# Gate loops of a fused graph network kernel: sigmoids in SBUF, two PSUM parts, query rows in PSUM

## The reference, cut to what matters

```python
def _gate(h, q, Wg, bg, Wq, bq):
    h3 = h.reshape(B, N, F)
    hg = jnp.einsum('bnf,gf->bng', h3, Wg[:, :F])
    qg = jnp.einsum('blf,gf->blg', q, Wg[:, F:]) + bg
    attn = jax.nn.sigmoid(hg[:, :, None, :] + qg[:, None, :, :])
    qi = jnp.einsum('bnlf,blf->bnf', attn, q)
    alpha = jax.nn.sigmoid(h3 @ Wq[:, :F].T + qi @ Wq[:, F:].T + bq)
    return (alpha * jnp.tanh(qi) + (1.0 - alpha) * h3).reshape(B * N, F)
```

## Time and profile before

| | |
|---|---|
| runs (3) | 1467.73 us median, 1459.67 to 1469.58 |
| the profiled execution | 1458.04 us, of it 1456.3 us span |
| TensorE matmul, busy | 1358.1 us (93%) |
| VectorE, busy | 986.9 us (68%) |
| ScalarE, busy | 773.1 us (53%) |
| GpSimd, busy | 207.3 us (14%) |
| mean granted TensorE clock | 0.974 |

### The profile page before, as it was taken

One profiled execution on the slowest core, in us unless ns is written; L12 is line 12 of the kernel. 1 busy time (PEld: TensorE's weight loads), 2 busy tenths in 40 slices (PEclk: granted clock), 3 DMA queues, 4 the chain that ended last, 5 costly groups with the idle time before them and its releaser, 6 DMA issues.

```text
span 1456.3 us, 24087 instructions
## 1 busy us (share of the span) xinstructions
PE 1358.1 (93%) x10014; PEld 1157.0 (79%) x10014; DVE 986.9 (68%) x1790; ACT 773.1 (53%) x1248; POOL 207.3 (14%) x103
## 2 busy tenths in 40 slices
PE   9999999999999798798789999789999999987998
PEld 8999433899533696588688999769899999986976
DVE  8745777645777756657667767776777677677455
ACT  3446888535888354344554654534455544445333
POOL 0110876000776100102001000001000000000100
PEclk9999999999999999999999999999999999998999
DMA  8456353146364222035325453063455555151100
GB/s 350 112 204 199 96 173 110 66 142 188 103 188 120 76 93 93 0 131 189 115 72 201 163 176 140 23 240 119 152 187 166 193 196 176 53 211 60 55 1 22
DMA packets 30835, 194.81 MB, mean 134 GB/s; under 512 B 4211, under 2 KB 4339, under 8 KB 14726
## 3 DMA queue, kind: packets, MB, share of 16 engines
q1 hardware_dynamic: 30726, 193.27, 39.0%
HBM read 183.03 MB, written 3.93 MB: 128 GB/s over the span
## 4 chain that ended last, share of the span: by engine, by line
PE 71%; DVE 17%; ACT 6%; POOL 3%; issue 2%; DMA 0%; DVEq 0%; SPq 0%; ACTq 0%; POOLq 0%
PE PS L358 55%; PE PS L978 6%; PE PS L987 5%; DVE WL L301 3%; PE PS L363 3%; POOL WK L1173 2%; PE PS L619 1%; POOL WL L308 1%; PE PS L460 1%; DVE SM L1345 1%; DVE SM L535 1%; DVE WK L1755 1%; ACT WH L294 1%; DVE WK L1760 1%; ACT GS L481 1%
## 5 line engine op out<-in xcount | busy, mean ns | idle before, releaser
L301 DVE TENSOR_TENSOR WL<-w,WH 128x768 fp32r<-128x768 f32 x373 | 354.6, 962 | 209.6 <-ACT WH L294 206.8
L294 ACT ACTIVATE WH<-w 128x768 fp32r<-128x768 f32 x381 | 315.5, 840 | 265.4 <-PE PS L358 252.3
L358 PE MATMUL PS<-XS,WH 128*128 128x256 f32 x2292 | 419.6, 286 | 13.0 <-DVE XS L485 7.1
L358 PEld LDWEIGHTS PS<-XS,WH 128*128 128x128 f32 x2292 | 357.2, 191 | 17.1 <-issue 11.1
L358 PE MATMUL PS<-XS,WL 128*128 128x256 f32 x1146 | 324.8, 283 | 0.0
L358 PEld LDWEIGHTS PS<-XS,WL 128*128 128x128 f32 x1146 | 218.5, 191 | 0.0
L1111 DVE TENSOR_TENSOR WK<-PS,WK 128x1024 f32<-128x1024 f32 x128 | 156.6, 1224 | 55.5 <-ACT PS L1055 54.5
L1173 POOL TENSOR_TENSOR WK<-WK 128x1024 f32<-128x1024 f32 x64 | 152.9, 2393 | 207.4 <-ACT WK L1052 207.4
L358 PE MATMUL PS<-WH,GS 128*128 128x256 f32 x864 | 159.0, 283 | 4.6 <-issue 1.4
L1055 ACT ACTIVATE PS<-PS 128x1024 f32<-128x1024 f32 x128 | 129.3, 1011 | 34.4 <-PE PS L978 34.3
L358 PEld LDWEIGHTS PS<-WH,GS 128*128 128x128 f32 x864 | 134.4, 188 | 7.3 <-issue 4.1
(11 more groups left out here) (253 smaller groups left out, 2014.2 us busy)
## 6 DMA issues: line engine op xcount, KB each, us to landing
w<-f2W_in SPq DMA_DIRECT2D x40, 1152.0 KB, 5.4
w<-Wrel_in SPq DMA_DIRECT2D x12, 1152.0 KB, 7.9
WK<-qrep_in SPq DMA_DIRECT2D x16, 768.0 KB, 5.5
w<-f1Wi_in SPq DMA_DIRECT2D x8, 1152.0 KB, 6.6
w<-f1Wo_in SPq DMA_DIRECT2D x8, 1152.0 KB, 5.1
w<-f3Wqkv_in SPq DMA_DIRECT2D x6, 1152.0 KB, 13.7
RT<-qg_rows SPq DMA_DIRECT2D x16, 384.0 KB, 6.2
RT<-AS SPq DMA_DIRECT2D x32, 192.0 KB, 6.6
```

Source lines behind the costliest of these rows:

```text
L294: A.e.activation(w_hi(i), w_raw(i), ACT.Copy).then_inc(*hi("w", i))
L301: V.e.tensor_tensor(w_lo(i), w_raw(i), w_hi(i), ALU.subtract).then_inc(*lo("w", i))
L358: ins = T.e.matmul(o, l, r, start=i == 0 and first, stop=i == n - 1 and last, skip_group_check=lint)
```

## The change

- The select parts get two places in PSUM instead of three: banks 4, 5 and 6, 7 in turn, `(3 * p + q) % 2`. A place is free as soon as ScalarE's sigmoid has read it.
- All three sigmoids write SG in SBUF. VectorE multiplies parts 0 and 2 in place there.
- VectorE's query rows lie in PSUM (GP, banks 2 and 3). For every group TensorE's new `spread(b)` fills them: two matmuls of 512 columns from QR, 64 partitions of XS (the two halves of 32 query rows), with the left side PK[0:64, 0:128]. It waits for VectorE's last product of the group before; VectorE's first product of a group waits for it.
- The split query rows come from DRAM (`query_rows`). Once, in the first graph layer, SyncE waits for the 32 stores, loads `qsel` (128 x 2048), ScalarE makes the upper half behind the aggregates of relation 2 and VectorE the lower, each one instruction, and SyncE stores them in 16 stores. This stands in `adj_sync`, ahead of `gate_sync` in the queue.
- The group's GQ load shrinks to GpSimd's 512 columns, and one load of QR is added.
- TensorE's order in the loop becomes select 0, sums unit 0, select 1, sums unit 1, select 2, and the spread of a group comes after select 2 of its first pair.

```diff
@@ -578,6 +579,7 @@
         qh, ql = (v[:, :].rearrange("p (k n) -> p k n", k=6) for v in (AS, XS))
         qgf = wk(14336, m=4, f=768)
         qgs = QS[:, :].rearrange("p (a m f) -> p a m f", a=2, m=4)
+        qss, qsx = QS[:, 0:4096].rearrange("p (a n) -> p a n", a=2), wk(4096, n=2048)
         Cr = wk(6144, r=3, m=2, n=256)
         Cj = wk(6144, j=6, n=256)
         Cn = wk(7680, n=512)
@@ -602,6 +604,15 @@
                         L.e.dma_start(qgr[2 * m + g // 2, a, :, g % 2, :],
                                       qgs[32 * g:32 * g + 32, a, m, :].bitcast(F32)).then_inc(*qg_out())
             qg_out.also("qg")
+            L.wait_ge(qg_out, "qg")
+            L.e.dma_start(qsx, dr["qsel"]).then_inc(*qs_in("qs"))
+            for a in range(2):
+                L.wait_ge(*((act, "upper", "qs"), (vec, "lower", "qs"))[a])
+                for g in range(4):
+                    for j in range(2):
+                        L.e.dma_start(qsr[4 * j + g, a, :, :],
+                                      qss[32 * g:32 * g + 32, a, 1024 * j:1024 * (j + 1)].bitcast(F32)).then_inc(*qs_out())
+            qs_out.also("qs")
 
         def adj_pe():
             b = bank_at(7, ("wake",), (pe, "wake"))
@@ -759,9 +770,11 @@
         NSG = 3
         SG = [wk(at, u=2, n=1536) for at in (0, 3072, 14336)]
         PARTS = [((0, 0), (0, 512)), ((0, 1024), (1, 1024)), ((1, 0), (1, 512))]
-        SP = [PS[:, 1024 * (1 + i):1024 * (2 + i)] for i in range(3)]
+        SP = [PS[:, 1024 * (2 + i):1024 * (3 + i)] for i in range(2)]
+        GP = PS[:, 1024:2048]
         GR = [RT[:, 1536 * i:1536 * (i + 1)] for i in range(2)]
-        GQ = [wk(11264 + 1536 * i, n=1536) for i in range(2)]
+        GQ = [wk(11264 + 512 * i, n=512) for i in range(2)]
+        QR = [XS[0:64, 1024 * (1 + i):1024 * (2 + i)] for i in range(2)]
         HG = AS[:, :].rearrange("p (a m f) -> p a m f", a=2, m=2)
         QA = wk(7680, n=384)
         QI = ((0, 224), (224, 256))
@@ -857,6 +870,8 @@
             for f in range(0, 6, 2):
                 aggregate(2, f)
             if n == "1":
+                A.wait_ge(qs_in, "qs")
+                act_upper(qss[:, 0, :], qsx, "qs")
                 A.wait_ge(pool, "counts")
                 A.e.activation(Cn, Cn, ACT.Ln).then_inc(*act())
                 A.e.activation(LD, LD, ACT.Ln).then_inc(*act("logs"))
@@ -895,6 +910,8 @@
             vec_gemm(t0, 12)
             for f in range(0, 6, 2):
                 aggregate(2, f)
+            if n == "1":
+                vec_lower(qss[:, 1, :], qsx, qss[:, 0, :], "qs")
             vec_gemm(t0, 24, None, 12)
             for f in range(6):
                 if f == 2:
@@ -916,9 +933,11 @@
             def queries(b):
                 if before(b) is not None:
                     o, d = before(b)
-                    for q in range(3):
-                        L.wait_ge(*prod(o, 4 * d + 3, q))
-                L.e.dma_start(GQ[b % 2], dr["qrep"][b]).then_inc(*qin[b % 2](n, b))
+                    L.wait_ge(*prod(o, 4 * d + 3, 1))
+                    L.wait_ge(pe, "gq" + o, d)
+                L.wait_ge(qs_out, "qs")
+                L.e.dma_start(GQ[b % 2], dr["qrep"][b]).then_inc(*qin[b % 2]())
+                L.e.dma_start(QR[b % 2].bitcast(F32), qsr[b].rearrange("a l n -> (a l) n")).then_inc(*qin[b % 2](n, b))
 
             def rows_q(b):
                 if before(b) is not None:
@@ -973,10 +992,16 @@
                     T.wait_ge(gin[b % 2], n, b)
                 for i, (u, c) in enumerate(PARTS[q]):
                     j = 2 * (p % 4) + u
-                    o = bank_at(2 + 2 * q + i, ("sg" + n, p, q, i),
-                                (act, "sig" + n, p, q) if q == 1 else (vec, "prod" + n, p, q))
+                    o = bank_at(4 + 2 * ((3 * p + q) % 2) + i, ("sg" + n, p, q, i), (act, "sig" + n, p, q))
                     ins = T.e.matmul(o, PK[:, j * P:(j + 1) * P], GR[b % 2][:, c:c + 512], start=True, stop=True)
                 ins.then_inc(*pe("sel" + n, p, q))
+
+            def spread(b):
+                T.wait_ge(qin[b % 2], n, b)
+                for i in range(2):
+                    o = bank_at(2 + i, ("gq" + n, b, i), (vec, "prod" + n, 4 * b + 3, 2))
+                    ins = T.e.matmul(o, PK[0:64, 0:P], QR[b % 2][:, 512 * i:512 * (i + 1)], start=True, stop=True)
+                ins.then_inc(*pe("gq" + n, b))
 
             def sums(p, u):
                 b, j = p // 4, 2 * (p % 4) + u
@@ -1002,6 +1027,7 @@
             T.wait_ge(act, "pick")
             gate_q(0)
             gate_q(1)
+            spread(0)
             select(0, 0)
             select(0, 1)
             gate_q(2)
@@ -1014,10 +1040,12 @@
             gate_q(5)
             for p in range(2, NPR):
                 select(p, 0)
+                sums(p - 2, 0)
                 select(p, 1)
-                sums(p - 2, 0)
+                sums(p - 2, 1)
                 select(p, 2)
-                sums(p - 2, 1)
+                if p % 4 == 0:
+                    spread(p // 4)
                 if p % 4 == 2 and p > 4:
                     turn_q(p // 4 - 1)
             for p in range(NPR - 2, NPR):
@@ -1047,12 +1075,13 @@
 
             def attend(p, q):
                 A.wait_ge(pe, "sel" + n, p, q)
+                free_sg(A, n, p)
+                o = SP[(3 * p + q) % 2]
                 if q == 1:
-                    free_sg(A, n, p)
-                    A.e.activation(SG[p % NSG][:, :, 1024:1536], SP[q].rearrange("p (u n) -> p u n", u=2),
+                    A.e.activation(SG[p % NSG][:, :, 1024:1536], o.rearrange("p (u n) -> p u n", u=2),
                                    ACT.Sigmoid).then_inc(*act("sig" + n, p, q))
                 else:
-                    A.e.activation(SP[q], SP[q], ACT.Sigmoid).then_inc(*act("sig" + n, p, q))
+                    A.e.activation(SG[p % NSG][:, q // 2, 0:1024], o, ACT.Sigmoid).then_inc(*act("sig" + n, p, q))
 
             feed_act(gh + 6)
             for m in range(2):
@@ -1106,10 +1135,9 @@
 
             def weigh(p, q):
                 V.wait_ge(act, "sig" + n, p, q)
-                V.wait_ge(qin[p // 4 % 2], n, p // 4)
-                free_sg(V, n, p)
-                V.e.tensor_tensor(SG[p % NSG][:, q // 2, 0:1024], SP[q], GQ[p // 4 % 2][:, 0:1024],
-                                  ALU.mult).then_inc(*vec("prod" + n, p, q))
+                V.wait_ge(pe, "gq" + n, p // 4)
+                g = SG[p % NSG][:, q // 2, 0:1024]
+                V.e.tensor_tensor(g, g, GP, ALU.mult).then_inc(*vec("prod" + n, p, q))
 
             feed_vec(gh + 6)
             for m in range(2):
@@ -1170,7 +1198,7 @@
                 s = SG[p % NSG][:, :, 1024:1536]
                 G.wait_ge(act, "sig" + n, p, 1)
                 G.wait_ge(qin[p // 4 % 2], n, p // 4)
-                G.e.tensor_tensor(s, s, GQ[p // 4 % 2][:, 1024:1536].unsqueeze(1).broadcast_to((P, 2, 512)),
+                G.e.tensor_tensor(s, s, GQ[p // 4 % 2].unsqueeze(1).broadcast_to((P, 2, 512)),
                                   ALU.mult).then_inc(*pool("prod" + n, p, 1))
                 if 4 <= p < 8:
                     feed_pool(qq_ + p - 3)
@@ -3019,7 +3047,9 @@
     a["edges"] = np.concatenate([i[k].reshape(P, NEDGE_T) for k in ("src", "dst", "edge_type_3")], 1)
     a["iota16"] = np.broadcast_to(np.arange(768, dtype=np.int16), (P, 768))
     q = i["L0_gnn_query_embs"].reshape(8, 2, 32, D)
-    a["qrep"] = np.tile(q.transpose(0, 2, 1, 3).reshape(8, 32, 2 * D), (1, 4, 1))
+    q = q.transpose(0, 2, 1, 3).reshape(8, 32, 2 * D)
+    a["qrep"] = np.tile(q[:, :, 1024:], (1, 4, 1))
+    a["qsel"] = q[:, :, :1024].reshape(2, 4, 32, 1024).transpose(1, 2, 0, 3).reshape(P, 2048)
     pick = np.zeros((P, 32, 32), np.float32)
     for l in range(32):
         pick[[l, 32 + l], :, l] = 1.0
```

More of the change, by code:

```diff
@@ L152, in wait_ge, with build @@
             self.seen[id(sem)] = value
-def build(nc, dr, out, qgr):
+def build(nc, dr, out, qgr, qsr):
     ctx = ExitStack()
@@ L201, in build @@
         pick_in, qg_out = newsem("pick_landed", 16), newsem("qg_stored", 16)
+        qs_in, qs_out = newsem("query_rows_landed", 16), newsem("query_rows_stored", 16)
         gin = [newsem(f"gate_rows_landed{i}", 16) for i in range(2)]
@@ L204, in build @@
         sems = [pe, act, vec, pool, hi, lo, log, *landed, *rowin, x_in, cols_in, edges_in, query_in, lora_in, stored,
-                pick_in, qg_out, *gin, *qin]
+                pick_in, qg_out, qs_in, qs_out, *gin, *qin]
         T, A, V, G, L = Port(pe), Port(act), Port(vec), Port(pool), Port()
@@ L3114 @@
     qgr = nc.dram_tensor("qg_rows", (8, 2, 32, 2, D), F32, kind="Internal").ap()
-    build(nc, dr, out, qgr)
+    qsr = nc.dram_tensor("query_rows", (8, 2, 32, 1024), F32, kind="Internal").ap()
+    build(nc, dr, out, qgr, qsr)
     r = _run(nc, [{k + "_in": v for k, v in arrays.items()}], core_ids=[0])
```

## The result

The changed kernel takes 1485.7 us (median of 4 runs, 1484.3 to 1487.7) against 1463.7 (1456.9 to 1469.6) for the kernel before in the same rounds: ratio 1.0153, 95% interval 1.0099 to 1.0206, so 22 us slower (14 to 30). Beside each other once more on another chip it was 1487.8 against 1462.2, ratio 1.0183 (1.0149 to 1.0217). The profiled execution took 1485.17, 27.1 more than that of before; its span is 1483.3.

A forecast was written before the change was run, and what follows sets the result against it. TensorE was taken as the bound, without waits in the gate loop. Detour 6.4 plus two gates 15.7 gave 22 us, so 1480 on the profile's footing of 1458.0; 5 more for timed runs gave 1485, range 1470 to 1499.

The forecast's parts named there:

- The 54 us of pauses are no waits: Gate loop: TensorE's weight-load pauses, ascribed to VectorE's products, are time in which sums stream; a pair stays 3.37 us.
- third rival: Gate loop: the pauses are waits after all, so the kernel gets faster, 36 us gained, 22 paid, 1449; chance 0.07.
- The order is worth 0: Gate loop: TensorE's new order has the same instructions and the same four changes between selects and sums; worth 0.
- Two parts instead of three: Gate loop: two PSUM parts barely fit, with cover of 0.12 and 0.13 us; cost 0.3 us a gate (0 to 1.6).
- second rival: Gate loop: ScalarE becomes the bound through slow release of PSUM to TensorE, 10 us more, 1495; chance 0.15.
- ScalarE's preparation, the start, the tail: Each gate: 1.0 us from ScalarE preparing weight tiles, 0.35 at the start, 0.5 at the end.
- The spread: Gates: TensorE's two 64-row matmuls cost 0.76 us (0.46 plus 0.3 for mode changes), eight times a gate.
- The 0.4 to be hidden once: Gate loop: ScalarE's weight preparation hides about 0.4 us of one spread, subtracted from the gate's sum.
- The detour: First graph layer: queued stores delay the third relation's weights; TensorE idles 4.4 and 0.4 us, clock loses 1.6; 6.4 us.
- The total: Whole kernel: 6.4 for the detour plus 15.7 for two gates, 22 us slower, 1485 us.
- The ends of the prediction's sum for a gate: Low and high ends of one gate's added time, 3.9 and 10.3 us, around the forecast 7.8.
- first rival: Whole kernel: cost stays small, spreads at 0.46, stores at 0.34, no clock loss; 10 us, 1475; chance 0.22.

The follow-up runs named there:

- a_nospread: Changed kernel with only the first group's spread of each gate kept, the other 14 left out; one run, 1473.8 us.
- a_oldorder: Changed kernel with TensorE's loop order of before (select 0, select 1, sums, select 2, sums); one run, 1480.0 us.
- a_full: Changed kernel with the spread's matmuls on all 128 rows, the lower 64 rows of XS zeroed by GpSimd; one run, 1481.0 us.
- a_late: Changed kernel with the 16 query-row stores moved behind the first gate's weight loads; 1480.2 us, ratio 1.0130 to the kernel before; once more 1477.1, ratio 1.0128.
- b_detour1: Kernel before with the query rows' detour alone (load, two halves, 16 stores), gates unchanged; 1467.7 us, ratio 1.0047.
- a_grouped: Changed kernel without spread and detour, VectorE's operands both in SBUF, three PSUM parts, all selects of a pair in a row; 1550.1 us, ratio 1.0602.
- a_sbufq: Changed kernel without spread and detour, VectorE's operands both in SBUF, two PSUM parts and new order kept; one run, 1566.8 us.

## Why the prediction was right, and where it was not

The forecast was 1485 with a range of 1470 to 1499, and 1485.7 was measured. The mechanism held: TensorE is the bound, nothing in the loop could gain, and the detour and most of the spreads' time (5.2 of 8 x 0.84 = 6.7 us a gate) are paid. Point by point:

- **The 54 us of pauses are no waits.** Right: the pair stayed at 3.37 to 3.38, and the pause kept its size with another name. The third rival (faster, 1449) falls with it.
- **The order is worth 0.** Right for a block without a spread (0.04, a_nospread). But the step looked at the changes between selects and sums alone, and not at where the spread would stand among them: inside a group of selects, which is 0.22 a block. With what ScalarE's preparation and the tail make of it the order costs 2.4 a gate (a_oldorder).
- **Two parts instead of three.** 0.3 a gate was forecast, 0.04 x 5 = 0.2 was found. The cover of 0.12 held, and the second rival (ScalarE the bound, 1495) falls: TensorE has no gap in any block.
- **ScalarE's preparation, the start, the tail.** Forecast 1.0, 0.35 and 0.5. Found in a_nospread: about 0.6 where selects wait for sigmoids, about 0.3 for the start, and 0.5 in the tail. Missing from the prediction is GpSimd: of the 0.9 in the pairs 6 to 10, 0.7 is a wait for its product, not for ScalarE. The prediction charged what happens in these pairs to the two parts; it belongs to the new order (a_oldorder, with two parts, has 0.35 there with its spread). With the two parts the forecast's terms came to 2.15; all that is not spread was 2.5. So the sum was nearly right, with a term too large for ScalarE and none for GpSimd.
- **The spread.** 0.76 was forecast, 0.84 measured in each of five blocks; the two changes of mode were sized at 0.3 from the earlier trace rows, and a_full has them at 0.40. The 0.4 to be hidden once was 1.4: in the pairs 6 to 10 a spread cost nothing (14.95 with, 14.97 without), since TensorE waited for GpSimd there anyway, and the one ahead of the first transpose 0.3 (29.29 with, 29.01 without). The first spread is 0.74, which is all that the first select moves against the gate's node product (17.93 against 17.19). Over a gate the eight came to 4.5 + 0.7 = 5.2, where 8 x 0.76 - 0.4 = 5.7 was forecast. These errors, and that of the term for GpSimd, offset each other: 7.7 a gate was measured, 7.8 was the forecast. That it came so close is luck.
- **The detour.** 6.4 was forecast, 6.9 to 9.0 measured in six executions. The order of the queue, the issue (106.9) and the duration of the stores (7.8 for 16) were right. Mis-sized were three terms. The tile that the copies push back costs 0.8 and not 0.4. The landing was taken as 5.7, the median of the earlier trace rows, and was 5.5 to 7.0. It comes at a moment when the loads of three matrices go out at once (the DMA engines are at 1.0 of their time in the stretches above); that this makes it long was not tested. The clock's 1.6 was 1.6 to 2.7, with half clock over 3.4 to 5.9 us of TensorE's work where the earlier trace rows had it for 1 and a part of 3.
- **The total.** 22 us was the sum, 27.1 the difference of the two profiles, 22.0 that of the medians. The sum of what the change does is 24.4 in the profile (up to the end of gate 2); the 4.5 of the attention stage belong to the execution (last section). With an interval of 14 to 30 the exact 22.0 is luck, the size is not. The ends of the prediction's sum for a gate, 3.9 and 10.3, come to about 4.2 and 10.2 by its own terms, which changes nothing. The first rival (the cost stays small, 1475) falls with 0.84 a spread and a clock at 0.50.

What stays open: why the same two loads land up to 1.5 us later in one execution than in another, what sets how long half clock outlasts the pause, and what in the attention stage makes the clock of one execution differ from the next.

## What to carry to other kernels

A pause that the trace ascribes to an engine is a wait only if the named work ended just before the pause did: look when it ended, and whether the same pause stands elsewhere with another cause. Freeing a buffer earlier is worth nothing on an engine that runs without a gap; each instruction added to that engine is paid in full wherever the engine has no wait to hide it in, and where it stands among changes of tile shape set a quarter of its price here. Ask which engine such a wait is for: here it was GpSimd, which none of the three rivals named. A store put into an ordered queue cost not its own time here but the lateness of the first load behind it, and on TensorE the clock's fall on top of the pause. Before a move of a few microseconds is read from single traces, take off what is already there ahead of the change: here up to 2.5 us.

## What the hardware showed that was not expected

- An untouched stage of the second layer (from the attention's first activation to the products behind it) took 91.5 us before, 96.0 and 92.9 in two executions of the changed kernel, 100.0 and 96.0 in two of a_late, with the same instructions. In all 13 traces it takes one of four lengths: 91.5 to 91.7 (3 of them), 92.7 to 92.9 (4), 96.0 to 96.1 (5, b_detour1 with the gates of before among them) and 100.0 (1). TensorE's granted clock differs in it. Its last 144 matmuls in before, after and a_late:

```profile
561.50:608.20 46.70, 34.65 (x144) 20.00 (x145) 35.50 (x101) 19.87 (x62) 6.84 (x2) 0.89 0.03 9
```

```profile
584.70:635.90 51.20, 39.65 (x144) 22.55 (x145) 35.91 (x101) 19.82 (x62) 6.85 (x2) 0.77 0.02 8
```

```profile
577.00:631.71 54.71, 44.32 (x144) 24.70 (x145) 35.79 (x100) 19.88 (x62) 6.85 (x2) 0.69 0.03 8
```

  VectorE and ScalarE are busy for the same time in all three; TensorE takes 34.7 to 44.3 us for the same matmuls. In the b_detour1 runs the time goes with the clock over the whole span: 1462.6 at 0.976 and 1479.0 at 0.962. A difference of under 10 us between two single executions of this kernel says nothing; landmarks up to that stage do, counted from the last one that the change can't have moved.
- VectorE and GpSimd together on SBUF: 1.22 us becomes 2.1 to 2.8 us for VectorE, while GpSimd goes from 2.39 (after) to 2.92 in a_grouped and stays at 2.4 in a_sbufq.
- A change of TensorE's tile from 128 to 64 rows and back costs 0.40 us in a row of 512-column matmuls, about as much as a change to 32 columns and back (0.35).
